# A graph network with hand-written queues: two program paths change places, and the work at their ends moves

## The reference

```python
def layer(x, W, b):                      # twice, with W0,b0 and W1,b1
    neigh = segment_sum(x[dst] / deg(src), src)      # rows=src, cols=dst
    return relu(concat([x, neigh]) @ W.T + b)
x = layernorm(x + layer(layer(x, W0, b0), W1, b1))
h = maxk(x @ W_neigh, 32)                # the 32 largest of each row stay
x = layernorm(x + x @ W_self + segment_sum(h[src], dst) / max(deg(dst), 1))
```

## Time and profile before

| what | value |
|---|---|
| median of three runs | 705.83 us |
| profiled execution, own time | 703.86 us |
| its span | 702.0 us |
| TensorE matmul busy | 639.5 us, 91% |
| VectorE / ScalarE / GpSimd busy | 502.3 / 353.3 / 106.9 us |
| start, up to `matched` | 0 to about 31 us |
| build | 31 to 193 us |
| first layer's sums | 193 to 385 us |

### The profile page before, as it was taken

One profiled execution on the slowest core, in us unless ns is written; L12 is line 12 of the kernel. 1 busy time (PEld: TensorE's weight loads), 2 busy tenths in 40 slices (PEclk: granted clock), 3 DMA queues, 4 the chain that ended last, 5 costly groups with the idle time before them and its releaser, 6 DMA issues.

```text
span 702.0 us, 11365 instructions
## 1 busy us (share of the span) xinstructions
PE 639.5 (91%) x4006; PEld 337.5 (48%) x4007; DVE 502.3 (72%) x1292; ACT 353.3 (50%) x678; POOL 106.9 (15%) x188
## 2 busy tenths in 40 slices
PE   7666788888788999999999999999999899999996
PEld 3345666666633444444444444444444344444443
DVE  6759989999748778888783578787787843634433
ACT  4698888899846676767673333333333210100000
POOL 3001222222111001010100222323222200000000
PEclk9999999999987999999999999999999999999999
DMA  8434554455431111111111555555656404310000
GB/s 209 94 91 131 178 169 141 142 167 166 147 91 37 30 39 36 39 35 39 36 37 41 160 171 168 168 176 157 185 153 184 117 31 137 117 48 22 23 27 26
DMA packets 39543, 73.09 MB, mean 104 GB/s; under 512 B 3120, under 2 KB 32207, under 8 KB 39481
## 3 DMA queue, kind: packets, MB, share of 16 engines
q1 hardware_dynamic: 39481, 72.30, 34.7%
HBM read 38.91 MB, written 33.38 MB: 103 GB/s over the span
## 4 chain that ended last, share of the span: by engine, by line
PE 72%; DVE 15%; ACT 7%; issue 2%; DMA 2%; SPq 1%; POOL 0%; ACTq 0%; DVEq 0%; POOLq 0%
PE pair L1577 36%; PE bank L1667 9%; PE pair L1667 8%; PE bank L1459 7%; DVE hots L640 6%; PE pair L1459 5%; PE bank L1451 2%; DVE ct L777 2%; ACT own L1122 2%; DVE x_t L770 2%; PE bank L1465 1%; ACT slab L1063 1%; DMA w_nat<-in_L_gnn_W_dram 1%; DMA own_in<-own_dram 1%; ACT x_t L1115 1%
## 5 line engine op out<-in xcount | busy, mean ns | idle before, releaser
L1577 PE MATMUL pair<-xs,ct 125*128 125x512 f16 x625 | 147.3, 388 | 0.0
L1577 PE MATMUL pair<-a,ct 125*128 125x512 f16 x625 | 142.8, 379 | 0.0
L640 DVE TENSOR_TENSOR hots<-iota,jobs 125x1792 f16<-125x1792 f16 (+1 forms) x100 | 104.6, 1063 | 5.8 <-PE pair L1370 5.2
L1577 PEld LDWEIGHTS pair<-xs,ct 125*128 125x128 f16 x625 | 62.3, 101 | 71.0 <-issue 6.0
L1577 PEld LDWEIGHTS pair<-a,ct 125*128 125x128 f16 x625 | 61.0, 99 | 68.1
L1063 ACT ACTIVATE slab<-pair 125x875 f16<-125x875 f32 (+1 forms) x100 | 83.3, 857 | 6.1 <-PE pair L1370 4.6
L1239 ACT ACTIVATE a<-ct 125x1000 f16<-125x1000 f16 (+1 forms) x75 | 80.2, 1069 | 6.8 <-DMA c_dram<-slab 5.9
L1667 PE MATMUL bank<-xs,ct 125*128 125x512 f16 (+1 forms) x325 | 71.5, 379 | 0.0
L1667 PE MATMUL pair<-xs,ct 125*128 125x512 f16 x300 | 66.5, 380 | 0.0
L1370 PE MATMUL pair<-hots 125*128 125x125 f16 x625 | 52.5, 223 | 14.7 <-ACT slab L1063 8.8
L1451 PE MATMUL bank<-ident,slab 125*128 125x125 f16 x625 | 51.9, 221 | 14.0 <-DVE ct L777 9.9
(11 more groups left out here) (215 smaller groups left out, 846.8 us busy)
## 6 DMA issues: line engine op xcount, KB each, us to landing
c_dram<-slab SPq DMA_DIRECT2D x25, 683.6 KB
ct<-c_dram SPq DMA_DIRECT2D x25, 683.6 KB
own_in<-own_dram SPq DMA_DIRECT2D x50, 125.0 KB
own_dram<-own SPq DMA_DIRECT2D x25, 125.0 KB
own_dram<-own_st SPq DMA_DIRECT2D x25, 125.0 KB
x_in<-in_x_dram SPq DMA_DIRECT2D x25, 125.0 KB
z_dram<-z_st SPq DMA_DIRECT2D x25, 125.0 KB
a<-z_dram SPq DMA_DIRECT2D x5, 625.0 KB
```

The costliest lines, as they stand in the source:

```text
L640: v.tensor_tensor(hots[k][:, :, :, :].rearrange("p w g (a d) -> p (w g) a d", d=2), iota, job, ALU.is_equal).then_inc(win_hot, 1)
L1577: ins = mm(agg[k % 3][0:lhs.shape[1], :], lhs, parts[l][:, t, :], start=t == 0, stop=t == NT - 1, skip_group_check=True)
```

## The change

1. **Order of the blocks.** On ScalarE and TensorE the quick block now stands first and the general one behind it, as it was on VectorE.
2. **Ends of the blocks.** TensorE's first sums (`layer_start`: the 50 matmuls of blocks 0 and 1) and VectorE's `sum_tree(0)` and `sum_tree(1)` (`first_trees`) are now written inside both blocks, at their ends. `invert(0)` follows after the join. `deg16` has two buffers, and the tree T waits for `degrees(T-2)`.
3. **ScalarE at the start of layer 1** does `h_high(0)` ahead of `degree(1, 1)` and `degree(1, 2)`.
4. **Own products.** Tiles 4 to 20 of the build carry one each, tiles 21 to 24 two each.
5. **Start.** The four sums of absolute values go from ScalarE to VectorE (one `tensor_reduce` each, ahead of `unpack(0)`). TensorE has 8 reader-less matmuls ahead of the wait for the weights and 4 instead of 6 behind their transposes. The transposes of the second weight matrix stand behind the four first fills, and ScalarE's copies of them and `square_x(1)` are reordered.

```diff
-OWN = {0: [], 1: [], 2: [], 3: [], 4: [0], 5: [1], 6: [2], 7: [3, 4], 8: [5], 9: [6, 7], 10: [8], 11: [9, 10], 12: [11],
-       13: [12, 13], **{t: [t] for t in range(14, NT)}}
+OWN = {**{t: [] for t in range(4)}, **{t: [t - 4] for t in range(4, 21)}, 21: [17, 18], 22: [19, 20], 23: [21, 22], 24: [23, 24]}
...
-        deg16 = lay("deg16", [P, 2, PC], F16)
+        deg16 = [lay(f"deg16_{i}", [P, 2, PC], F16) for i in range(2)]
...
+            dve.wait_ge(w_loaded, 32)
+            dve.wait_ge(const_ready, 10)
+            for l in range(2):
+                for h in range(2):
+                    at = 6 + 2 * l + h
+                    v.tensor_reduce(stat[:, at:at + 1], w_nat[:, l, h, :], X, ALU.add, apply_absolute_value=True).then_inc(w_sums, 1)
             unpack(0)
...
+            def first_trees():
+                for free in tr_free:
+                    dve.wait_ge(free, 2 * NT + 1)
+                sum_tree(0)
+                sum_tree(1)
...
                 for g in (1, 3):
                     tr_copy(NT - 1, g)
+                first_trees()
...
-            sum_tree(0)
             invert(0)
-            sum_tree(1)
...
-            act.wait_ge(w_loaded, 32)
-            act.wait_ge(const_ready, 11)
-            for l in range(2):
-                for h in range(2):
-                    at = 6 + 2 * l + h
-                    a.activation(junk[:, :], w_nat[:, l, h, :], ACT.Abs, accum_out=stat[:, at:at + 1]
-                                 ).then_inc(act_step, 1)
-                    act.wait_ge(act_step, 2 * l + h + 1)
-            act.sem_inc(act_sums, 1)
...
             quick_copy(0, 0)
             quick_copy(0, 1)
+            square_x(1)
+            quick_copy(0, 2)
             weights_out(1, 0)
             weights_out(1, 1)
-            quick_copy(0, 2)
-            square_x(1)
             jobs_out(1)
...
             act.wait_ge(matched_ready, 1)
             total = act.value_load(matched[0:1, 0:1], min_val=0, max_val=E)
+            with act.If(total > E - 1):
+                quick_copies()
             with act.If(total < E):
...
-            with act.If(total > E - 1):
-                quick_copies()
...
+                if T == 0:
+                    h_high(0)
                 if T + 1 < NT:
                     degree(T + 1, 1)
                     degree(T + 1, 2)
-                h_high(T)
+                if T:
+                    h_high(T)
...
+            keep_clock(bank[3], 8)
             pe.wait_ge(w_loaded, 32)
...
-            keep_clock(bank[3], 6)
+            keep_clock(bank[3], 4)
...
-            fill(0, 0)
+            pe.wait_ge(wt_copied, 2)
+            for f in range(FILLS):
+                fill(0, f)
+                if f < FILLS - 1:
+                    keep_clock(bank[7], KEEP[0])
             for h in range(2):
-                pe.wait_ge(wt_copied, h + 1)
                 weights_t(1, h)
-            for f in range(1, FILLS):
-                fill(0, f)
-                if f == 1:
-                    pe.wait_ge(wt_copied, 4)
-                keep_clock(bank[7], KEEP[0])
...
+            def layer_start():
+                pe.wait_ge(a0_split, NT)
+                for free in tr_free:
+                    pe.wait_ge(free, 2 * (NT - 1) + 1)
+                aggregate(0, 0, 0, NT - 2)
+                aggregate(0, 1, 0, NT - 2)
+                for free in tr_free:
+                    pe.wait_ge(free, 2 * NT + 1)
+                pe.wait_ge(a0_split, NT + 2)
+                for T in range(2):
+                    aggregate(0, T, NT - 2, NT)
+
             total = pe.value_load(matched[0:1, 0:1], min_val=0, max_val=E)
+            with pe.If(total > E - 1):
+                fills()
+                layer_start()
             with pe.If(total < E):
...
-            with pe.If(total > E - 1):
-                fills()
+                layer_start()
+
             degrees(0)
             aggregate(0, 2, 0, 9)
             degrees(1)
```

More of the change, by code:

```diff
@@ L213, in gnn @@
         w_nat = pre("w_nat", [128, 2, 2, 2 * F], F32)
-        junk = pre("junk", [128, 2 * F], F32)
         lay = Arena(shared_at, nc.sbuf_usable_end)
@@ L792, in general_hots, with sum_tree, step @@
                                         ALU.is_equal).then_inc(hot_ready, 1)
+            def sum_tree(T):
+                count = [8 * T]
+                def step(ins):
+                    count[0] += 1
+                    ins.then_inc(tree_step, 1)
+                    dve.wait_ge(tree_step, count[0])
+                quint = [region[T][:, 5 * PC * k:5 * PC * (k + 1)] for k in range(5)]
+                step(v.tensor_tensor(tree[:, :], quint[0], quint[1], ALU.add))
+                for k in range(2, 5):
+                    step(v.tensor_tensor(tree[:, :], tree[:, :], quint[k], ALU.add))
+                step(v.tensor_tensor(tree2[:, :], tree[:, 0:2 * PC], tree[:, 2 * PC:4 * PC], ALU.add))
+                step(v.tensor_tensor(tree2[:, 0:PC], tree2[:, 0:PC], tree[:, 4 * PC:5 * PC], ALU.add))
+                step(v.tensor_tensor(tree2[:, 0:PC], tree2[:, 0:PC], tree2[:, PC:2 * PC], ALU.add))
+                if T > 1:
+                    dve.wait_ge(deg_done, T - 1)
+                step(v.tensor_copy(deg16[T % 2][:, 0, :], tree2[:, 0:PC]))
+                v.tensor_tensor(deg16[T % 2][:, 1, :], tree2[:, 0:PC], deg16[T % 2][:, 0, :], ALU.subtract).then_inc(deg_split, 1)
+            def first_trees():
[3 more added lines that the diff above has]
+                sum_tree(1)
             dve.wait_ge(matched_ready, 1)
@@ L823, in _ @@
                     tr_copy(t - 1, 3)
-                    if len(own) > 1:
+                    if len(own) > 1 and own[1] + 1 < NT:
                         own_low(own[1] + 1)
@@ L1164, in quick_copies @@
                         own_copy(own[1], own[1] % 2, own[1] // 2)
-                        own_t(own[1] + 1)
+                        if own[1] + 1 < NT:
+                            own_t(own[1] + 1)
                     if 2 < t < 5:
@@ L1409, in bounds_t @@
                 pe.wait_ge(stat_ready, 2)
-                pe.wait_ge(act_sums, 1)
+                pe.wait_ge(w_sums, 4)
                 pe.wait_ge(wt_copied, 4)
@@ L1506, in fills @@
                 pe.wait_ge(tr_cleared, 2)
+                pe.wait_ge(wt_copied, 4)
                 for t in range(1, NT):
@@ L1542, in fills @@
                         own_product(own[1], 1)
-                        own_transposes(own[1] + 1, xs32[:, own[1] + 1, :])
+                        if own[1] + 1 < NT:
+                            own_transposes(own[1] + 1, xs32[:, own[1] + 1, :])
                     transposes(t - 1, par, 3)
@@ L1608, in degrees @@
                     pe.wait_ge(deg_ready, T)
-                mm(bank[7][0:P, T:T + 1], deg16[:, 0, 0:P], ones16[:, :], start=True, stop=False, skip_group_check=True)
-                mm(bank[7][0:P, T:T + 1], deg16[:, 1, 0:P], ones16[:, :], start=False, stop=True, skip_group_check=True
+                mm(bank[7][0:P, T:T + 1], deg16[T % 2][:, 0, 0:P], ones16[:, :], start=True, stop=False, skip_group_check=True)
+                mm(bank[7][0:P, T:T + 1], deg16[T % 2][:, 1, 0:P], ones16[:, :], start=False, stop=True, skip_group_check=True
                    ).then_inc(deg_done, 1)
-            pe.wait_ge(a0_split, NT)
-            for free in tr_free:
-                pe.wait_ge(free, 2 * (NT - 1) + 1)
-            aggregate(0, 0, 0, NT - 2)
-            aggregate(0, 1, 0, NT - 2)
-            for free in tr_free:
-                pe.wait_ge(free, 2 * NT + 1)
-            pe.wait_ge(a0_split, NT + 2)
-            for T in range(2):
-                aggregate(0, T, NT - 2, NT)
+            def layer_start():
[9 more added lines that the diff above has]
+                    aggregate(0, T, NT - 2, NT)
+            total = pe.value_load(matched[0:1, 0:1], min_val=0, max_val=E)
+            with pe.If(total > E - 1):
+                fills()
+                layer_start()
+            with pe.If(total < E):
+                pe.wait_ge(win_read, FILLS - 1)
+                general_table()
+                bounds_t()
+                bounds_row()
+                scales_b()
+                windows()
+                transposes(NT - 1, 0, 0)
+                own_transposes(NT - 1, xs32[:, NT - 1, :])
+                transposes(NT - 1, 0, 1)
+                transposes(NT - 1, 0, 2)
+                transposes(NT - 1, 0, 3)
+                own_product(NT - 1, 0)
+                own_product(NT - 1, 1)
+                layer_start()
             degrees(0)
```

4 lines of the change are left out of this document (2 added, 2 removed).

## The result

The changed kernel takes 699.74 us (median of 13 runs, 695.69 to 701.27), the kernel before 705.64 (13 runs). The ratio is 0.9904, 95% interval 0.988 to 0.9929: 6.8 us faster, between 5.0 and 8.5. The ratio goes by the means; the two medians alone differ by 5.9. The forecast was 7.2. The total is right, but its terms are not: the own products gave next to nothing instead of 1.2, the trees gave about a third of their 2.6, and two amounts came that the prediction did not have (the table in "Why the prediction was right").

A forecast was written before the change was run, and what follows sets the result against it. Engines passing over the general block stood idle 2.3 to 7.3 us, at the path choice or the build's end. Gains of 3.8 (entry and start), 1.2 and 2.2 made 7.2 us: 705.83 to 698.6 us, range 695.3 to 703.6.

The forecast's parts named there:

- Own products: Part 3, build tiles: late double tiles, the last one's second product costing 0.7 instead of 1.9 us; gain 1.2 us.
- The entry: Part 1, from `matched` at 31 us: TensorE and ScalarE enter the quick path without the jump; gain 3.1 us.
- The start: Part 2, before `matched`: sums hidden in VectorE's idle time, `unpack(0)` at 17.35 instead of 18.06; gain 0.7 us.
- Three of the four cost the same: Build: of four double tiles, three cost 1.9 us extra as before; only tile 24 differs.
- Trees and `h_high(0)`: Start of layer 1: both trees run beside the 50 matmuls, `degrees(3)` at 219.6 instead of 222.19; gain 2.6 us.
- TensorE's jump: At the join behind the 50 matmuls: mostly covered because the queue runs ahead; cost 0.4 us.
- part 2: The start's edits; the prediction said the fetch rule spoke against it, through new branches at the join; gain 0.7 us.
- part 4: Trees and the join at the start of layer 1: 2.6 us less 0.4 for TensorE's jump; gain 2.2 us.
- bare jump of TensorE: Rival, at the join: uncovered jump makes `degrees(0)` 4.9 to 5.1 us later; net gain 2.6, 703.2 us; chance 0.17.
- VectorE's jump is long again: Rival, at the join: VectorE's or ScalarE's jump is long; net 5.2, 700.6 us; chance 0.22 with the smaller early gain.
- The early gain is smaller: Rival, first tiles: only 2.3 of 3.8 us arrive; net 5.7, 700.1 us; chance 0.22 shared with the long jump.
- The slower rival: TensorE's jump stays at the entry and comes again at the exit; 0.5 to 2.7 us slower; chance 0.06.

The follow-up runs named there:

- e1_order_only: The kernel before with one edit: on TensorE and ScalarE the quick block stands first; 707.75 us, ratio 1.0037 to the kernel before.
- e3_ends_behind: The changed kernel with TensorE's 50 first sums and VectorE's first two trees behind the join; 705.27 us, ratio 1.0003 to the kernel before.
- c1_after_again: The changed kernel measured again without any edit; 699.2 us, ratio 0.9913 to the kernel before.
- e2_own_before: The changed kernel with the own-product table of the kernel before (double tiles 7, 9, 11, 13); 699.88 us, ratio 0.9907 to the kernel before.
- e4_pad32: The changed kernel with 32 no-operations in VectorE's jumped-over general block; 696.51 us, ratio 0.987 to the kernel before.
- e9_warm10: The changed kernel with 32 no-operations in VectorE's unused block, double tiles 7, 22, 23, 24, and 10 instead of 4 reader-less matmuls before the picks; 694.29 us.
- e7: The changed kernel with only VectorE's first two trees behind the join; 701.2 us, ratio 0.9936 to the kernel before.

## Why the prediction was right, and where not

- **The jump moves, and its cover decides.** Shown. e1_order_only moves it without cover and is slower than before; e3_ends_behind takes the cover away and loses 6 us.
- **The entry** was put at 3.1 of the 3.8 us. It is 3.6 for TensorE (5.08 to 1.47) and 3.9 for ScalarE (4.78 to 0.86). The step that failed is "the table load of 1.28 stays, since ScalarE loads one in each block": with the quick block first there is none at the entry. My 0.3 for the register load was too short in exchange; the copy comes 0.86 after `matched`. That ScalarE then carries the whole gain through the first tiles held only where tile 2 had the full clock. From `matched` to the first fill of tile 4 it was 28.76 us before, 24.86 in e3_ends_behind (3.9 won), but 26.09 in c1_after_again (2.7 won).
- **The start** was put at 0.7 and gave 1.06 where the picks had the full clock (c1_after_again; the kernel before had 0.95 there). In the profile after it gave -1.56. The four reductions took 2.46 us together, near the 2.7 counted, and were hidden. What I did not put in the range was that the granted clock in the picks differs from execution to execution.
- **Own products** were put at +1.2 and cost 1.1 to 1.4 in the build. Two steps failed. "Three of the four cost the same" overlooked what the double tile 7 covered, a wait of ScalarE for the weights' store (1.3 to 1.6 us in tile 8). And the last tile's second product costs 1.6 us, not 0.7: from its first fill to the first sum it is 192.21 - 181.84 = 10.37 against 8.75 before. A third thing was not in the sum: with that second product the 50 sums keep the full clock and take 10.96 instead of 12.53 us (e2_own_before). Both together make the part about 0.2 us (e2_own_before, to `degrees(0)`), so it is neither the gain forecast nor a loss.
- **Trees and `h_high(0)`** were put at 2.6. Without the code gap the chain from `degrees(0)` to `degrees(3)` falls from 17.08 to 14.54 us (e4_pad32), 2.5. In the changed kernel as it is, it falls only to 16.1 to 16.3, since the gap of 1.8 to 1.9 us lies in it. The `degrees(0)` of before:

```profile
205.11 0.17 PE L1609 MATMUL bank<-ones,deg 125*125 125x1 f16 x1
```

- **TensorE's jump** was put at 0.4 and cost nothing here (0.78 in one profile of e9_warm10). That the queue runs ahead of the matmuls is thereby borne out, since e3_ends_behind shows the same jump bare at 5.44. Where the prediction says that the fetch rule speaks against part 2, it means part 4, the join.
- The rival "bare jump of TensorE" is excluded. "VectorE's jump is long again" did not happen; ScalarE's was long (5.7 to 6.0 us), but with `h_high(0)` moved ahead nothing waited for it, and 1.8 us of a second gap came on VectorE. "The early gain is smaller" came true in part (the profile after: 1.65 us by tile 4). The slower rival is excluded by the entry.

The stretches of the program, one behind the other, in the profile before and in c1_after_again (us):

| stretch | forecast gain | before | c1_after_again | gain |
|---|---|---|---|---|
| up to `matched` | 0.7 | 31.13 | 30.07 | 1.06 |
| to the first fill of tile 4 | 3.1 | 28.76 | 26.09 | 2.67 |
| to the first sum | 1.2 | 132.86 | 134.23 | -1.37 |
| to `degrees(0)` | -0.4 | 12.36 | 10.79 | 1.57 |
| to `degrees(3)` | 2.6 | 17.08 | 16.27 | 0.81 |
| to the end of the span | 0 | 479.81 | 478.45 | 1.36 |
| together | 7.2 | 702.0 | 695.9 | 6.1 |

The last gain is none of the change's that any run shows: nothing was edited there, and in the thirteen profiles this stretch takes 477.4 to 480.2 us. So the total was right partly by luck. What stood behind it (the entry, the covered jump) held; of the rest, a wait, a code gap and the clock in tile 2 took away about as much as the clock of the sums and the last stretch gave.

## What to carry to other kernels

A program with a path that is not taken pays for passing over it, and an engine pays at the place where that block stands: put such a jump behind work that is already queued and whose waits are met, and it costs next to nothing (0 to 0.78 us here instead of 5.4). When work is moved to a later step, look first for what the old place covered; a wait that does not show in the profile can be the price. Look then at what follows the new place: here a busier TensorE just ahead of the long sums kept their clock up, 1.6 us that repaid the price. An issue gap just behind a jump may only be the place of the code, and a few dead instructions can move it away.

## What the runs showed of the hardware

- Passing over the unused block shows as 2.3 us of idle time on ScalarE and 5.1 on TensorE at 31 us, with the DMA at 0.04. At the build's end, beside the slab stores, it is 5.4 to 5.5 on TensorE with nothing queued (e1, e3), 5.7 to 6.0 on ScalarE in the changed kernel and 7.3 to 8.2 on VectorE (before, e1, e3, e7).
- Code that never runs changed the timeline: 32 no-operations took away a gap of 1.8 us.
- TensorE's granted clock in the picks (14 to 25 us) differed with the same products there, and `matched` followed it in all thirteen profiles: 29.89 to 30.50 us at 1.00 (seven), 31.13 at 0.95, 31.86 at 0.84, 32.69 at 0.69, and 34.60 to 35.40 at 0.60 to 0.55 (three). What decides it was not found.
- The 50 sums took 10.95 or 10.96 us in the nine profiles with two products in the last tile and the sums ahead of the join (TensorE busy 2.92 or 2.93 of the 4 us before). They took 12.53 and 12.64 us with one product there (before and e2, busy 2.13), and 12.53 and 12.96 behind a bare jump (e3 and e1, idle). In these four the granted clock was 0.50 to 0.60 in the first 4 us of the sums.
